# Cross-attention with tokens on partitions: maxima subtracted in PSUM, exponentials transposed on TensorE, one 9-column product a head

## The reference

```python
gate = sigmoid(depthwise_conv1d(x_t, gate_w, gate_b))      # 7 taps
cand = tanh(depthwise_conv1d(x_t, cand_w, cand_b))
h = decay_scan(gate * cand, exp(log_decay))                # along the tokens
y = h.T @ out_w.T + out_b + x
x = layernorm(x + y * rsqrt(mean(y * y) + RMS_EPS) * norm_w)

q, k, v = x @ Wq + bq, ctx @ Wk + bk, ctx @ Wv + bv        # 16 heads of 8
scores = where(causal, q @ k.T / sqrt(8), lowest) + mask
out = softmax(scores) @ v
x = layernorm(x + out @ Wp + bp)

g = moe_linear(x, router_gate, w_gate)                     # 8 experts, the best 2 a token
u = moe_linear(x, router_up, w_up)                         # 128 -> 512
d = moe_linear(silu(g) * u, router_down, w_down)           # 512 -> 128
x = layernorm(x + d)
```

## Time and profile before

| | before |
|---|---|
| median of the runs | 319.29 us |
| span of the profiled execution | 317.6 us |
| PE busy | 284.1 us (89%), 1,899 instructions |
| PE weight loads (PEld) | 206.0 us (65%) |
| DVE busy | 198.8 us (63%) |
| ACT busy | 85.8 us (27%) |
| POOL busy | 106.1 us (33%) |
| mean granted TensorE clock | 0.923 |
| moved by DMA | 10.03 MB |

### The profile page before, as it was taken

The page is one execution under the profiler, slowest core; times in us unless marked ns, Lnnn a source line. Parts: engine busy times, 40 slices in busy tenths (PEclk is TensorE's granted clock), DMA queues, the critical chain, the costliest instruction groups (busy, mean ns, idle before and its releaser), DMA issues.

```text
span 317.6 us, 4970 instructions
## 1 busy us (share of the span) xinstructions
PE 284.1 (89%) x1899; PEld 206.0 (65%) x1899; DVE 198.8 (63%) x550; ACT 85.8 (27%) x150; POOL 106.1 (33%) x120
## 2 busy tenths in 40 slices
PE   6549978477987989999999999999999999999992
PEld 2235544244765758787876777777778778788771
DVE  4985573664157667548774963696568748653374
ACT  3603646113221612421141115211411312221010
POOL 4562755542202740640334036003602420410001
PEclk9958976655699999999999999999999999999999
DMA  7932254000000000000000000000000000000000
GB/s 220 343 106 83 75 178 155 0 2 0 1 2 0 3 0 3 0 2 0 2 8 2 1 10 0 0 2 8 3 0 2 8 2 0 11 1 10 0 0 17
DMA packets 5553, 10.03 MB, mean 32 GB/s; under 512 B 917, under 2 KB 3349, under 8 KB 5525
## 3 DMA queue, kind: packets, MB, share of 16 engines
q1 hardware_dynamic: 4666, 8.77, 8.4%
q10 hardware_dynamic: 864, 0.94, 0.9%
HBM read 9.19 MB, written 0.52 MB: 31 GB/s over the span
## 4 chain that ended last, share of the span: by engine, by line
PE 74%; DVE 16%; issue 3%; POOL 2%; ACT 2%; DMA 1%; POOLq 0%; SPq 0%; DVEq 0%
PE PS L893 26%; PE PS L941 13%; PE PS L717 5%; PE PS L869 5%; PE PS L710 4%; PE PS L825 3%; PE PS L802 3%; PE PS L836 3%; PE PS L797 2%; DVE CAND L1024 2%; PE PS L839 2%; PE PS L814 2%; DVE ROOM L1205 2%; PE PS L916 2%; DMA XT<-x_t 1%
## 5 line engine op out<-in xcount | busy, mean ns | idle before, releaser
L893 PE MATMUL PS<-WH,XH 128*128 128x512 f32 x128 | 57.7, 451 | 0.0
L557 POOL TENSOR_TENSOR ROOM<-X,CGU 128x512 f32<-128x512 f32 x32 | 33.2, 1040 | 58.7 <-DVE CGU L1149 38.5
L893 PE MATMUL PS<-WH,XL 128*128 128x512 f32 x128 | 51.2, 400 | 0.0
L893 PE MATMUL PS<-WL,XH 128*128 128x512 f32 x128 | 51.1, 399 | 0.0
L1156 DVE TENSOR_TENSOR XL<-PS,XH 128x512 fp32r<-128x512 f32 x32 | 22.0, 687 | 30.6 <-ACT XH L662 30.4
L662 ACT CAST XH<-PS 128x512 fp32r<-128x512 f32 x32 | 18.8, 586 | 58.7 <-PE PS L869 58.7
L893 PEld LDWEIGHTS PS<-WH,XL 128*128 128x128 f32 x128 | 24.4, 190 | 5.8
L893 PEld LDWEIGHTS PS<-WH,XH 128*128 128x128 f32 x128 | 24.3, 190 | 5.0 <-issue 0.6
L893 PEld LDWEIGHTS PS<-WL,XH 128*128 128x128 f32 x128 | 24.7, 193 | 2.4
L492 POOL TENSOR_SCALAR ZR<-ZMV 128x1 f32<-128x1 f32 x8 | 2.4, 300 | 70.3 <-DVE ZMV L1111 70.3
L540 POOL TENSOR_SCALAR_AFFINE_SELECT PT<-PT 128x1024 f32<-128x1024 f32 x16 | 18.1, 1134 | 22.3 <-ACT PT L645 22.3
(11 more groups left out here) (165 smaller groups left out, 512.7 us busy)
## 6 DMA issues: line engine op xcount, KB each, us to landing
ROOM<-w_gate SPq DMA_DIRECT2D x4, 512.0 KB, 8.4
ROOM<-w_up SPq DMA_DIRECT2D x4, 512.0 KB, 4.0
ROOM<-w_down SPq DMA_DIRECT2D x4, 512.0 KB, 4.6
RO<-rows SPq DMA_DIRECT2D x1, 516.0 KB, 7.8
X<-x_tok ACTq DMA_DIRECT2D x1, 512.0 KB, 3.9
XT<-x_t SPq DMA_DIRECT2D x2, 256.0 KB, 6.2
CT<-ctx_t SPq DMA_DIRECT2D x1, 512.0 KB, 5.8
y_out<-ROOM SPq DMA_DIRECT2D x8, 64.0 KB, 1.5
```

What stands on the lines that cost most here:

```text
L557: g.tensor_tensor(XE[:, k % 2, :, :], X[:, t, None, :].broadcast_to([P, 4, P]), CGU[:, t, r, 4 * q:4 * q + 4, None].broadcast_to([P, 4, P] ...
L893: last = mm(PS[:, product_bank(t, r), :], a[:, r, cut], w[:, r, e * I:(e + 1) * I], start=e == 0 and n == 0, stop=e == E - 1 and n == 2)
```

## The change

The scores are made once. DVE takes the maximum of each token and head and subtracts it from the scores where they lie, in PSUM. ACT takes the exponential to SBUF (`PQ`), still with tokens on partitions; a masked score becomes 0 there, so POOL clears nothing. PE transposes the exponentials, 128x128 each, back into the same bank pair (step ST), and ACT copies them to SBUF (`PT`). The values get a ninth column of ones for each head (`VA`), so one product of 9 columns a head gives the weighted values and their denominator, with tokens on partitions. DVE divides (`ON`), and a new step OT transposes the outcome on PE and copies it on ACT ahead of the output product. Steps NM, A and VM are gone, POOL's part of ST as well. The tables that place the steps, and the list of the start, are written anew:

```diff
-EARLY = [('WM', 9), ('GC',), ('AX',), ('GT', 0), ('W', 0), ('W', 1), ('O', 0), ('RD',), ('N1', 0), ('C1',), ('C1',), ...
+EARLY = [('WM', 9), ('GC',), ('K', 0), ('AX',), ('GT', 0), ('W', 1), ('W', 0), ('O', 0), ('C1',), ('N1', 0), ('C1',), ...
-TILE_AT = [1.0, 6, 3, 4.5, 7.5, 10, 11, 12.5, 12.5, 14, 15, 16.5, 17.5, 20.0, 18.0, 20.5]
-PAIR_AT = [6.5, 6.5, 8.5, 9.5]
+TILE_AT = [2.6, 4.6, 6.6, 8.6, 14.6, 9.6, 20.6, 10.6, 21.6, 13.6, 15.0, 19.6, 17.0, 21.0]
+PAIR_AT = [5.0, 5.0, 9.0, 9.0]
...
-    steps = [("A", t), ("VM", nxt), ("ST", t, 0), ("ST", t, 1), ("PV", t, 0), ("PV", t, 1), ("S", nxt, 0), ("WO", t),
-             ("S", nxt, 1), ("N2", t), ("NM", nxt), ("X2", t), ("LG", t), ("V", t + 2), ("XE", 4 * t),
-             ("XE", 4 * t + 1)]
+    steps = [("ST", t, 1), ("PV", t, 0), ("PV", t, 1), ("OT", t), ("S", nxt, 0), ("WO", t), ("ST", nxt, 0),
+             ("N2", t), ("S", nxt, 1), ("X2", t), ("LG", t), ("V", t + 2), ("XE", 4 * t), ("XE", 4 * t + 1)]
...
+@@ ACT @@
+                elif what == "S":
+                    t, p = args
+                    act.wait_ge(d_sub, 2 * t + p + 1)
+                    if t or p:
+                        act.wait_ge(pe_st, 2 * t + p)
+                    b = pair_bank(*x)
+                    s.activation(PQ[:, :, :, :].rearrange("q s g k -> q (s g k)"), flat(PS[:, b:b + 2, :]), ACT.Exp)\
+                        .then_inc(a_exp, 1)
                 elif what == "ST":
...
-                    s.activation(PT[:, 2 * p:2 * p + 2, :, :].rearrange("k s g q -> k (s g q)"),
-                                 PS[:, b:b + 2, :].rearrange("k s c -> k (s c)"), ACT.Exp).then_inc(a_exp, 1)
+                    s.copy(PT[:, 2 * p:2 * p + 2, :, :].rearrange("k s g q -> k (s g q)"), flat(PS[:, b:b + 2, :]))\
+                        .then_inc(a_pt, 1)
+                elif what == "OT":
...
+                    s.copy(OT[:, :], PS[:, ONE, 2 * P:3 * P]).then_inc(a_ot, 1)
...
 @@ PE @@
                elif what == "ST":
...
-                            last = mm(PS[:, b + s, g * P:(g + 1) * P], KS[r:r + 32, g, c],
-                                      QSA[r:r + 32, g, :], start=True, stop=True)
+                    for s in range(2):
+                        for g in range(NG):
+                            last = transpose(PS[:, b + s, g * P:(g + 1) * P], PQ[:, s, g, :], ID[:, :])
...
                 elif what == "PV":
...
                         for g in range(NG):
-                            mm(PS[32 * g:32 * g + 32, ONE, 0:P], VM[:, t % 2, s, 32 * g:32 * g + 32], PT[:, s, g, :],
-                               start=s == 0, stop=s == NS - 1, skip_group_check=True)
-                        for g in range(NG):
-                            last = mm(PS[32 * g:32 * g + 32, ONE, P:2 * P],
-                                      RO[:, R_HM + s * P + 32 * g:R_HM + s * P + 32 * g + 32], PT[:, s, g, :],
-                                      start=False, stop=s == NS - 1, skip_group_check=True)
+                            h = NS * g + s
+                            last = mm(PS[:, ONE, h * (DH + 1):(h + 1) * (DH + 1)], PT[:, s, g, :], VA[:, t % 2, h, :],
+                                      start=True, stop=True)
@@ DVE, S and PV @@
-                    v.tensor_reduce(NM[:, 2 * p:2 * p + 2, :], PS[:, b:b + 2, :]
-                                    .rearrange("q s (g k) -> q s g k", g=NG), AX_X, ALU.max, negate=True)\
-                        .then_inc(d_max, 1)
+                    v.tensor_reduce(NM[:, 2 * p:2 * p + 2, :], scores, AX_X, ALU.max).then_inc(d_max, 1)
+                    dve.wait_ge(d_max, 2 * t + p + 1)
+                    v.tensor_tensor(scores, scores, NM[:, 2 * p:2 * p + 2, :, None].broadcast_to([P, 2, NG, P]),
+                                    ALU.subtract).then_inc(d_sub, 1)
...
+                    heads = PS[:, ONE, 0:HEADS * (DH + 1)].rearrange("q (h d) -> q h d", d=DH + 1)
+                    link(v.reciprocal(RC[:, :], heads[:, :, DH]))
+                    v.tensor_tensor(ON[:, :].rearrange("q (h d) -> q h d", d=DH), heads[:, :, 0:DH],
+                                    RC[:, :, None].broadcast_to([P, HEADS, DH]), ALU.mult).then_inc(d_on, 1)
```

More of the change, by code:

```diff
@@ L224, in decoder_layer @@
         KS = sb("KS", [P, NG, W2], F32R)
-        QSA = sb("QSA", [P, NG, P], F32R)
-        VB = sb("VB", [P, 2, P])
-        VM = sb("VM", [P, 2, NS, P])
+        VA = sb("VA", [P, 2, HEADS, DH + 1])
         NM = sb("NM", [P, NS, NG])
-        NMS = sb("NMS", [P, NG, P])
+        PQ = sb("PQ", [P, 2, NG, P])
         PT = sb("PT", [P, NS, NG, P])
-        RC = sb("RC", [P, P])
+        RC = sb("RC", [P, HEADS])
+        ON = sb("ON", [P, P])
         OT = sb("OT", [P, P])
@@ L337, in decoder_layer @@
         a_exp = sem("a_exp")
+        a_pt = sem("a_pt")
+        a_ot = sem("a_ot")
         a_x2 = sem("a_x2")
@@ L351, in decoder_layer @@
         d_st = sem("d_st")
-        d_vb = sem("d_vb")
+        d_va = sem("d_va")
         d_max = sem("d_max")
-        d_nms = sem("d_nms")
-        d_qsa = sem("d_qsa")
-        d_ot = sem("d_ot")
+        d_sub = sem("d_sub")
+        d_on = sem("d_on")
         d_z = sem("d_z")
@@ L805, in _ @@
                     last.then_inc(pe_s, 1)
-                elif what == "A":
-                    t, = args
-                    pe.wait_ge(d_nms, t + 1)
-                    pe.wait_ge(d_vb, min(t + 2, B))
-                    if t == B - 1:
-                        pe.wait_ge(d_lg, t)
-                    for g in range(NG):
-                        last = transpose(PS[:, ONE, g * P:(g + 1) * P], NMS[:, g, :], ID[:, :])
-                    last.then_inc(pe_aug, 1)
                 elif what == "ST":
                     t, p = args
-                    pe.wait_ge(d_qsa, t + 1)
                     b = free_pair(*x)
-                    c = tile_of_pair(t)
-                    for g in range(NG):
-                        for s in range(2):
-                            r = 32 * (2 * p + s)
-                            last = mm(PS[:, b + s, g * P:(g + 1) * P], KS[r:r + 32, g, c],
-                                      QSA[r:r + 32, g, :], start=True, stop=True)
+                    pe.wait_ge(a_exp, 2 * t + p + 1)
+                    for s in range(2):
+                        for g in range(NG):
+                            last = transpose(PS[:, b + s, g * P:(g + 1) * P], PQ[:, s, g, :], ID[:, :])
                     last.then_inc(pe_st, 1)
@@ L830, in _ @@
                     t, p = args
-                    pe.wait_ge(p_sel, 2 * t + p + 1)
+                    pe.wait_ge(a_pt, 2 * t + p + 1)
                     if p == 0:
-                        pe.wait_ge(p_vm, t + 1)
+                        pe.wait_ge(d_va, min(t + 2, B))
+                        if t:
+                            pe.wait_ge(d_lg, t)
                     for s in (2 * p, 2 * p + 1):
                         for g in range(NG):
-                            mm(PS[32 * g:32 * g + 32, ONE, 0:P], VM[:, t % 2, s, 32 * g:32 * g + 32], PT[:, s, g, :],
-                               start=s == 0, stop=s == NS - 1, skip_group_check=True)
-                        for g in range(NG):
-                            last = mm(PS[32 * g:32 * g + 32, ONE, P:2 * P],
-                                      RO[:, R_HM + s * P + 32 * g:R_HM + s * P + 32 * g + 32], PT[:, s, g, :],
-                                      start=False, stop=s == NS - 1, skip_group_check=True)
+                            h = NS * g + s
+                            last = mm(PS[:, ONE, h * (DH + 1):(h + 1) * (DH + 1)], PT[:, s, g, :], VA[:, t % 2, h, :],
+                                      start=True, stop=True)
                     last.then_inc(pe_pv, 1)
+                elif what == "OT":
+                    t, = args
+                    pe.wait_ge(d_on, t + 1)
+                    transpose(PS[:, ONE, 2 * P:3 * P], ON[:, :], ID[:, :]).then_inc(pe_ot, 1)
                 elif what == "WO":
@@ L846, in _ @@
                         pe.wait_ge(ld_q, 32)
-                    pe.wait_ge(d_ot, t + 1)
-                    mm(PS[:, ONE, 2 * P:3 * P], OT[:, :], WP[:, :], start=True, stop=True).then_inc(pe_wo, 1)
+                    pe.wait_ge(a_ot, t + 1)
+                    mm(PS[:, ONE, 0:P], OT[:, :], WP[:, :], start=True, stop=True).then_inc(pe_wo, 1)
                 elif what == "X2":
```

66 lines of the change are left out of this document (19 added, 47 removed).

## The result

The changed kernel takes 348.49 us, the median of four runs (347.62 to 351.53), against 319.15 us of the kernel before: a ratio of 1.094 with a 95% interval of 1.090 to 1.098. It is slower by 9.4%, and the forecast of 349.5 us holds. Its profiled execution has a span of 346.7 us. Some executions run disturbed, at a lower granted clock; medians further down are those of the others, and from the two profiles of such executions (without the subtraction, and with a split moved) only durations and waits of single instructions are read.

What follows compares the result with a forecast made beforehand. PE's work was taken to bound full tiles, with half clock and idle time before them; 12.1 (start) + 15.2 + 2.9 = 30.2 us on the 317.6 span, plus 1.7 to the median, gave 349.5 us, range 338 to 356.

Steps and rivals of the forecast that it cites:

- sixteen 9-column products: PE's work in a full tile: 32 float32 passes at 0.11 us each, set by the stationary load, 3.5 us.
- wait for ITL: Full tile: PE's down-router product waits some 1.9 us for DVE's low part of the inner activations.
- wait for the copy ahead of second scores: Full tile: the second pair's scores wait 0.55 us for ACT's copy of the first pair's transposes, sharing one bank pair.
- wait for the copied outcome: Full tile: PE's output product waits 0.3 us for ACT's copy of the transposed outcome.
- four full stretches: From the down-router product of 123.4 us on: 3.6 us more each, plus 0.4 in two of them, +15.2 us.
- fifth stretch: Last stretch with attention: work, two copy waits and a score product of 1.24 us that used to lie earlier, +2.9 us.
- start: Up to the first down-router product: +3.0 us to the first expert product, +9.1 from there; 12.1, bounds -4 and +18.
- Rival (D): Values products in every tile go by their columns: 0.3 us a tile for 3.5, total 324 us; chance 0.03.
- Rival (A): Only PE's work counts; DVE and ACT absorb the added operations, waits are nothing, total 326 us; chance 0.09.
- one small subtraction of the router: Start: a 2.20 us DVE operation no longer runs beside a POOL split; first expert inputs a good 1 us earlier.
- Rival (B): Start: tile 0 reaches its router early, the first expert product comes at 68 us at best, total 315; chance 0.06.
- rival (C): Start: worse, at half clock through the key projection and beyond, with unfound waits, 10 us more, 360; chance 0.09.

## Why the prediction was right, point by point

| step | predicted, us | measured, us |
|---|---|---|
| sixteen 9-column products | 3.5 a tile | 3.5: twice 183.88 - 181.64 - 0.47 |
| sixteen transposes | 1.76 | 1.74: twice 180.70 - 178.93 - 0.47 - 0.43 |
| wait for ITL | 1.9, four times | 1.64, 1.65, 1.64, 1.86 listed |
| wait for the copy ahead of second scores | 0.55 | 0.50 listed, five times |
| wait for the copied outcome | 0.3 | none listed; 0.2 by starts in three of five tiles |
| four full stretches | +15.2 | +15.6 |
| fifth stretch | +2.9 | +3.1 |
| behind it | 0 | 0.0 |
| start | +12.1 | +10.4 |
| span | +30.2 | +29.1 |

**Work.** That a pass of 9 columns costs as much as one of 128 was read from the router product, and it held to a few hundredths. Rival (D), by columns, is out. The reason that I gave, the load, fits so far as half the load is faster; but ahead of the run with halves I took the price for a fixed one of each pass, which it refuted.

**Waits.** The wait for ITL was found by laying the new order on DVE's durations, and it fell within 0.3 us; the run with the order mended took it away. Rival (A), that engines with room absorb the additions, was wrong for the reason given: the room lay behind ITL. A listed wait begins at the modelled end of the pass before, and so misses a part. From start to start, as the work was computed, ITL costs 202.60 - 200.55 - 0.235 = 1.8, the copy 174.09 - 173.20 - 0.235 = 0.65 and the copied outcome 190.11 - 189.68 - 0.235 = 0.2 (ACT's copy runs from 189.78 to 190.05). With 0.8 of work these are the 3.5 us of the tile: here the prediction was right term by term.

**The start.** The sum was 1.7 us too high, and its parts were further off: +3.7 for +3.0 up to the first expert product, +6.7 for +9.1 from there. That the whole span came within 1.1 us is in part luck, as these errors cancel. The step "one small subtraction of the router ... no longer meets that split, and the first expert inputs come near 65.0" failed: the split met another operation of DVE, the normalization ahead of it, which took 2.36 us for 0.35, and the inputs came at 67.4. I had asked which operation leaves the collision, not which one comes into it. The first scores came at 42.23, not 40.4. Against these, the values product took 3.7 us and not 5.0, and the way from the inputs to the first expert product took 12.6 and not 14.3. On that way the second scores took 1.2 us and not 2.0 (from 72 to 75 us PE had its full clock, where I had counted on half). So that product came at 79.96 for 79.3 predicted. From there the waits were 10.7 us for 12.75: 2.5 for the normalized row (2.6), 4.0 for the copy (4.65), 2.2 for the exponentials (3.1), 1.7 around the inner activations (1.9). The clock took its part: from 105 to 117 us, around the waits of 4.0 and 2.2, PE has 0.57 of its clock, where before it had all. The first row is of the changed kernel, the second of before:

```profile
105.00:117.00 12.00, 7.47 (x31) 5.36 (x32) 3.50 (x6) 4.44 (x11) 2.00 (x4) 0.57 0.01 1
```

```profile
105.00:117.00 12.00, 10.82 (x121) 7.73 (x120) 8.04 (x19) 3.81 (x5) 8.51 (x9) 1.00 0.01 2
```

Rival (B), an early start, is out by the first expert product (80.0, and it needed 72); rival (C), 10 us more, as well.

## What to carry to other kernels

Where one list sets the order on all engines, lay the new order on the old durations and add them up to each instruction that the busiest engine waits for; an engine's idle share says nothing about that, the place of its idle time does. Price a small product by a row with the same load, not by its columns, and when the load is what costs, try half the stationary columns. In a chain that is late as a whole, taking away the wait with the largest number only gives its time to the next one.

## What the runs showed of the hardware

- Float32 passes with 9 streamed columns start 0.115 us apart with 128 stationary columns, and 0.035 with 64 in the two halves of the array in turn; with 64 so and 128 streamed columns, 0.068.
- A VectorE operation of 0.35 us took 2.28 to 2.37 in every run of the changed order in which GpSimd split a chunk beside it, and 0.34 or 0.35 in both runs in which it did not. The Trainium skill (SBUF — State Buffer, Who interferes with whom) says that VectorE and GpSimd share a pair of ports, which one of them can hold for a whole instruction while the other waits; the trace agrees, since the short operation ends with the split (63.27 and 63.19).
- A reciprocal took 1.76 us for 256 columns on 32 partitions, and 0.95 for 128 columns on 128 (in the kernel before).
- An exponential of 128 columns that sums as it goes costs ACT 0.35 us, where 1,024 columns at once cost 1.03.
